# State space: moving sixteen token gathers one chunk later and splitting their statistics in two batches

## What is computed

```python
xn = x * rsqrt(mean(x * x) + EPS) * norm_w
xi, res = split(xn @ in_proj_w)
xi = silu(conv(xi) + conv_b)
delta, Bm, Cm = split(xi @ x_proj_w)
delta = softplus(delta @ dt_proj_w + dt_proj_b)
A = -exp(A_log)
# over the tokens of a sequence, 256 channels by 16 states:
state = exp(delta * A) * state + delta * Bm * xi
y = sum over states of state * Cm
out = (y + xi * D) * silu(res) @ out_proj_w + x
```

## Time and profile before

| what | value |
|---|---|
| median of 3 runs | 1254.69 us (1253.68 to 1259.11) |
| the profiled launch | 1261.0 us, its span 1259.1 us |
| DVE busy | 942.2 us (75%) |
| PE busy | 998.2 us (79%) |
| POOL busy | 830.8 us (66%) |
| ACT busy | 735.4 us (58%) |
| the state-space stage, first `dBu` to last `gate_rows` | 472.9 to 969.5 us |

### The profile page before, as it was taken

One profiled execution on the slowest core, in us unless ns is written; L12 is line 12 of the kernel. 1 busy time (PEld: TensorE's weight loads), 2 busy tenths in 40 slices (PEclk: granted clock), 3 DMA queues, 4 the chain that ended last, 5 costly groups with the idle time before them and its releaser, 6 DMA issues. The chain is left out here.

```text
span 1259.1 us, 17033 instructions
## 1 busy us (share of the span) xinstructions
PE 998.2 (79%) x4202; PEld 606.3 (48%) x4202; DVE 942.2 (75%) x2310; ACT 735.4 (58%) x1636; POOL 830.8 (66%) x604
## 2 busy tenths in 40 slices
PE   5888867489999978888888888898776335999970
PEld 4666755368888723333333333333222333777750
DVE  6999999653333437999898989999998743777760
ACT  4777747265555568776667676867531113777740
POOL 3333248557247275989898978787975077767676
PEclk9999989599999979999898989989989556999995
DMA  9993012246435343353544443444542014756543
GB/s 271 177 168 124 1 10 24 40 60 92 73 77 94 69 80 104 111 170 116 164 125 153 137 124 126 160 130 140 168 150 67 2 49 76 120 104 123 106 93 64
DMA packets 139137, 133.50 MB, mean 106 GB/s; under 512 B 14579, under 2 KB 120163, under 8 KB 138915
## 3 DMA queue, kind: packets, MB, share of 16 engines
q1 hardware_dynamic: 107106, 115.55, 34.2%
q0 software_dynamic: 31936, 16.86, 11.4%
HBM read 98.66 MB, written 31.60 MB: 103 GB/s over the span
## 5 line engine op out<-in xcount | busy, mean ns | idle before, releaser
L1871 POOL TENSOR_TENSOR ss_HC<-ss_Hs,ss_Cb 128x512 f32<-128x512 f32 x256 | 324.8, 1365 | 85.0 <-PE ss_Y L1621 64.4
L1621 PE MATMUL ss_Y<-ss_HC,g_ident 128*128 128x512 f32 x512 | 270.4, 649 | 47.3 <-POOL ss_HC L1871 41.0
L1915 DVE TENSOR_TENSOR_SCAN ss_Hs<-ss_dA,ss_dBu 128x512 f32<-128x512 f32 x256 | 296.8, 1200 | 7.7 <-ACT ss_dA L1781 7.7
L846 POOL DMA_INDIRECT rows<-m_XS,g_slot x128 | 174.3, 1362 | 61.7 <-issue 34.6
L1781 ACT ACTIVATE ss_dA<-ss_delta,g_A 128x510 f32<-128x510 f32 x256 | 168.3, 712 | 74.1 <-DVE ss_Hs L1915 73.9
L1621 PEld LDWEIGHTS ss_Y<-ss_HC,g_ident 128*128 128x128 f32 x512 | 92.9, 200 | 209.2 <-POOL ss_HC L1871 149.2
L1153 PE MATMUL m_x_UP<-g_m_w,m_x_gT 128*128 (+1 forms) x532 | 193.0, 469 | 0.0
L1907 DVE TENSOR_TENSOR ss_dBu<-ss_duP,ss_Bb 128x512 f32<-128x512 f32 x256 | 163.1, 682 | 10.5 <-DMA ss_Bb<-bc_rows 8.9
L1173 PEld LDWEIGHTS m_x_DP<-g_m_w,m_x_hT 128*128 128x128 f32 x908 | 121.9, 191 | 62.3 <-issue 34.6
L1173 PE MATMUL m_x_DP<-g_m_w,m_x_hT 128*128 (+1 forms) x908 | 140.7, 284 | 2.4 <-ACT m_x_hT L1245 2.3
L1245 ACT ACTIVATE m_x_hT<-m_x_HP 128x256 f32<-128x256 f32 (+1 forms) x188 | 80.3, 427 | 87.7 <-PE m_x_HP L1163 85.9
(11 more groups left out here) (271 smaller groups left out, 1760.9 us busy)
## 6 DMA issues: line engine op xcount, KB each, us to landing
ss_Bb<-bc_rows SPq DMA_DIRECT2D x64, 512.0 KB, 5.0
ss_Cb<-bc_rows SPq DMA_DIRECT2D x64, 512.0 KB, 4.1
rows<-g_Z SPq DMA_DIRECT2D x2, 5031.0 KB, 48.9
m_x_G<-rows SPq DMA_DIRECT2D x156, 64.5 KB
out_rows<-m_x_YO SPq DMA_DIRECT2D x156, 64.0 KB
g_m_w<-in_w_up SPq DMA_DIRECT2D x1, 2816.0 KB, 11.2
g_m_b<-in_b SPq DMA_DIRECT2D x1, 2160.0 KB, 10.3
g_X<-in_x SPq DMA_DIRECT2D x4, 512.0 KB, 5.8
```

Source lines behind the costliest of these rows:

```text
L846: self.nc.gpsimd.indirect_dma_start(self.XG, bass.IndirectOffsetOnAxis(self.rt.slot[k][:, t:t + 1], 0), self.XS[:, t, :], None, compute_op ...
L1621: ins = nc.tensor.matmul(Yp[:, h, :], ident[:], HC[n % 2][:, h, :], start=False, stop=n == N - 1)
L1871: nc.gpsimd.tensor_tensor(HC[n % 2][:, h, :], Hs[n % 4][:, h, :], Cb[g % 2][:, n % 2, :], ALU.mult).then_inc(hc_ready.sem, 1)
L1915: v_.tensor_tensor_scan(Hs[n % 4][:, h, :], dA[n % NA][:, h, :, :].rearrange("p s t -> p (s t)"), dBu[:, h, :], 0.0, ALU.mult, ALU.add).th ...
```

## The change

The 16 gathers of the last eight tiles move one chunk later. Before, POOL issued the eight with the first expert's rows in chunks 0 and 1 and the eight with the second expert's in chunks 2 and 3. Now tiles 24 to 27 get theirs in chunk 1 (first expert) and chunk 2 (second), and tiles 28 to 31 in chunks 3 and 4. The eight tiles become two batches of four, each with a semaphore of its own. The first has statistics at (4, 1), root at (4, 2), scales at (4, 3); the second has them at (5, 1), (5, 2) and (5, 3). SP's increment of a semaphore that nobody waits for, one per chunk, goes.

```diff
@@ state_space
-        gathered, late_gathered = m.sem("gathered"), m.sem("late_gathered")
-        soon, late = rows_of.batches[1], rows_of.batches[2]
-        n_soon, n_late = soon[1] - soon[0], late[1] - late[0]
-        sp_passed = m.sem("sp_passed")
+        gathered, late_gathered = m.sem("gathered"), [m.sem(f"late_gathered{q}") for q in range(2)]
+        soon, late = rows_of.batches[1], rows_of.batches[2:]
+        n_soon, n_late = soon[1] - soon[0], G
@@ SP
                     if back:
                         sp.wait_ge(bc_stored.sem, bc_stored.after(c + 1))
-                        sp.sem_inc(sp_passed, 1)
@@ ACT
-                        if (c, n) == (4, 2):
-                            rows_of.scalar_root(act, 2)
+                        if c in (4, 5) and n == 2:
+                            rows_of.scalar_root(act, c - 2)
@@ POOL
-                        i = 4 * c + (n - 8) // 2
-                        if n >= 8 and n % 2 == 0 and i < 2 * n_late:
-                            if i == n_late:
-                                pool.wait_ge(late_gathered, 16 * n_late)
-                            gather(i // n_late, late[0] + i % n_late, late_gathered)
+                        if 1 <= c <= 4 and n >= 8 and n % 2 == 0:
+                            q, k = divmod(c - 1, 2)
+                            if k == 1 and n == 8:
+                                pool.wait_ge(late_gathered[q], 16 * n_late)
+                            gather(k, late[q][0] + (n - 8) // 2, late_gathered[q])
@@ DVE
-                        if (c, n) == (4, 1):
-                            dve.wait_ge(late_gathered, 16 * 2 * n_late)
-                            rows_of.vector_stats(dve, 2, *late)
-                            rows_of.vector_moments(dve, 2)
-                        if (c, n) == (4, 3):
-                            rows_of.vector_scales(dve, 2)
+                        if c in (4, 5) and n == 1:
+                            dve.wait_ge(late_gathered[c - 4], 16 * 2 * n_late)
+                            rows_of.vector_stats(dve, c - 2, *late[c - 4])
+                            rows_of.vector_moments(dve, c - 2)
+                        if c in (4, 5) and n == 3:
+                            rows_of.vector_scales(dve, c - 2)
@@ build
-        state_rows = StateRows(nc, Maker(nc, outer, "sr_"), chain, X, mean, scales, ((0, HT), (HT, HT + 8), (HT + 8, T)))
+        state_rows = StateRows(nc, Maker(nc, outer, "sr_"), chain, X, mean, scales, ((0, HT), (HT, HT + 8), (HT + 8, HT + 12), (HT + 12, T)))
```

## The result

The changed kernel takes 1263.61 us in the median of 20 runs (1258.53 to 1271.88). The kernel before, run beside it, takes 1255.44 us (1252.41 to 1265.18, 20 runs). The ratio is 1.0051 with a 95% interval of 1.0034 to 1.0067: 6.4 us slower on 1254.69, or some 1261.1 us. The two medians lie 8.2 us apart, but each list spreads over 13 us, so I go by the ratio and its interval. The kernel is slower, since the interval leaves out 1. Whether by more than the 0.5% at which the prediction parted "slower" from "within" isn't decided: the ratio is just beyond it, and the interval holds it. The forecast was +5.7 us.

What follows compares the result with a forecast made beforehand. DVE was taken to bound the stage. Statistics in chunk 5 (+1.6) and the second root and scales (+4.1) made +5.7 us on 1254.69, so 1260.4 us, 0.45% slower; the range ran from 1255.5 to 1264.5.

Steps and rivals of the forecast that it cites:

- Chunk 0 buys nothing: Chunk 0: four gathers removed from POOL gain 0, since DVE never waited for POOL; bounds 0 and a 6.8 us gain.
- Chunks 1 to 3 at 0: Chunks 1 to 3: four gathers each as before and the same order on every engine, so 0 us.
- a sign against it: Periods of chunks 0 to 3 changing by over 1 us would show the prediction wrong.
- the moments are held up: Rival at (5, 1): POOL runs on through it and adds 3.2 us; +8.9, 1263.6 us; chance 0.10.
- Chunk 4, gathers hidden: Chunk 4, steps 8 to 14: four more POOL gathers hide under DVE's work; the sum is ready at 800.7.
- Statistics in chunk 5, +1.6: Chunk 5, step 1: statistics for a batch of four on DVE cost +1.6 us, bounds 0.4 and 2.5.
- POOL falls behind in chunk 4: Rival: PE's waits do not cover the first two gathers, sum 3.4 us later; +7.9, 1262.6 us; chance 0.15.
- Second root and scales, +4.1: Chunk 5, steps 2 and 3: 7.4 us on DVE, partly given back, leaving +4.1; bounds 2.5 and 7.4.
- chunks 6 and 7 keep their periods: Chunks 6 and 7: no change in their periods; all that follows the stage moves along.
- The sum: Whole kernel: 1.6 + 4.1 = +5.7 us, 1260.4 us, 0.45% slower.
- The port: Chunk 5's scales: blocked by POOL's instruction under the shared port rule, they stay at 2.8 us; without it 1.3.

Runs made afterwards that it cites:

- e2: The kernel before with the four gathers of chunk 0 left out (tiles 24 to 27 lack the first expert's rows); ratio 0.9997.
- e1: The changed kernel with its two batches, but every gather at its old step in chunks 0 to 3; ratio 1.0024 against the kernel before.
- e9: The kernel before with ACT's root behind its gate copy at (4, 3), DVE's scales at (4, 5) and chunk 6's normalise at step 5; ratio 0.9999.
- e3: The kernel before with four more gathers at steps 8 to 14 of chunk 4, into a tile nobody reads, without SP's increments; ratio 1.0011.
- e6: The changed kernel with both late roots ahead of the logarithm in ACT's step 2 instead of behind it; ratio 1.0052 against the kernel before.
- e10: The changed kernel with both late roots behind ACT's gate copy, scales and normalise at step 5 in chunks 4 and 5; ratio 1.0122 against the kernel before.
- e4: The changed kernel without the second root and second group of scales, chunk 7 normalised with constants; ratio 1.0038 against the kernel before.
- e11: The changed kernel without the second root only; the seven scale operations stay, chunk 7 uses chunk 6's numbers; ratio 1.0034 against the kernel before.
- e5: The kernel before with ACT's late root ahead of the logarithm in step 2 of chunk 4 instead of behind it; ratio 1.0007.
- e7: The kernel before with DVE's late scales at (4, 5) instead of (4, 3), and ACT's normalise of chunk 6 at step 5; ratio 1.0010.

## Why the prediction was nearly right

**Chunk 0 buys nothing.** Right. First `dBu` to first `gate_rows` took 78.21 us (548.15 - 469.94) instead of 78.44, and e2's ratio is 0.9997 with an interval that leaves out the 6.8 us.

**Chunks 1 to 3 at 0.** Wrong for chunks 1 and 2. The prediction had named a change of over 1 us there as a sign against it, and chunk 1 grew by 1.58. Chunks 1 and 2 together take 124.65 us after the change, and 124.64 to 124.78 in all four other launches that have both its gathers and its split. In six launches without that combination they take 122.62 to 122.81, e2 among them, and in two (e1, e9) 123.9. What goes with it in all thirteen launches is PE's clock. Here are the two chunks together, of the changed kernel, of e9 and of the kernel before:

```profile
548.15:672.80 124.65, 108.24 (x245) 43.79 (x246) 113.32 (x133) 83.41 (x125) 108.18 (x80) 0.92 0.44 137
```
```profile
551.36:675.28 123.92, 107.14 (x247) 43.51 (x246) 113.64 (x133) 84.87 (x128) 109.04 (x80) 0.93 0.46 141
```
```profile
551.33:674.14 122.81, 106.08 (x248) 44.04 (x248) 113.51 (x133) 85.16 (x128) 109.77 (x81) 0.94 0.46 140
```

A granted clock of 1.00 is 2.4 GHz throughout; less is a stretch with a part at 1.2 GHz. Summed from the clock's records, PE spends 20.5 us of the two chunks at 1.2 GHz in the five launches of 124.6 to 124.8 us, 17.1 in the two of 123.9 and 13.7 in the six of 122.6 to 122.8. DVE is busy for the same time in all (113.3 to 113.6 us), so the difference is waiting. Against the kernel before, most of it is one wait for B in the middle of chunk 1, 2.61 us instead of 1.15:

```profile
585.57 1.30 DVE L1905 TENSOR_TENSOR ss_dBu<-ss_duP,ss_Bb 128x512 f32<-128x512 f32 x2 [2.61 <-DMA ss_Bb<-bc_rows]
```
```profile
587.28 1.30 DVE L1907 TENSOR_TENSOR ss_dBu<-ss_duP,ss_Bb 128x512 f32<-128x512 f32 x2 [1.15 <-DMA ss_Bb<-bc_rows]
```

The rest is the wait for the sum, 3.57 instead of 3.21 us in chunk 1 and 3.48 instead of 3.08 in chunk 2. Against e2 it is the other way round: there the wait for B is 2.35 and the wait for the sum only 2.57. The eight `ss_HC` products before the next `gate_rows` show why, first in the changed kernel, then in the kernel before, then in e2:

```profile
599.46 5.76 PE L1619 MATMUL ss_Y<-ss_HC,g_ident 128*128 128x512 f32 x8 [1.87 <-POOL ss_HC L1869]
```
```profile
601.43 5.40 PE L1621 MATMUL ss_Y<-ss_HC,g_ident 128*128 128x512 f32 x8 [1.87 <-POOL ss_HC L1871]
```
```profile
608.35 4.79 PE L1621 MATMUL ss_Y<-ss_HC,g_ident 128*128 128x512 f32 x8 [1.89 <-POOL ss_HC L1871]
```

In the first two a part of the products runs at 1.2 GHz, in e2 none does. So where the slow stretches fall decides which wait grows, and how long they are in all goes with how long the chunks take. That the clock is the cause and no mere companion is argued from the products' times, not shown: no run sets it. The changed kernel and e2 have the same granted clock in each ten microseconds from 20 us before `gate_rows` to 50 us behind it, and PE is busy within 0.4 us of the same time in each. Why it then falls in one and not in the other isn't settled. e2 shows that fewer gathers in chunk 0 do not do it alone. e9, which before chunk 4 runs the same order of work as the kernel before, shows that one order can come out two ways.

In chunk 3's window, which holds the statistics of (4, 1), the 0 was right: 62.16 us against 62.38 and 62.12. But nothing came earlier, for the batch of four took 3.76 us to the next `dBu`, more than the 3.29 of the eight tiles before. Its L1408, which takes 0.17 us in chunk 5, took 2.42 here and ended at 733.70, with POOL's run of products (733.66). So the rival "the moments are held up" came true in a place where it cost nothing.

**Chunk 4, gathers hidden.** Right for the window (e3: 63.98 against 63.77, and no wait of DVE for the sum behind it). The sum was ready 64.1 us after `gate_rows` in the changed kernel and 63.9 in e3, against the forecast's 800.7 - 736.52 = 64.2. But the prediction asked only whether POOL would make `gate_rows` late. It didn't ask what else ran ahead of DVE at that point. e1 shows it: the second root is waited for 1.31 us without these gathers, and 3.98 with them.

**Statistics in chunk 5, +1.6.** Right: 1.52 in the row, +1.48 in the window, and the four other launches with the full change's gathers give 64.76 to 65.29. The moments ran free of POOL here, so that rival did not come true in chunk 5, though it was close: in e6 and e10 the same batch took 2.8 us there. The rival in which POOL falls behind in chunk 4 is out, because DVE didn't wait before `gate_rows` at 800.21.

**Second root and scales, +4.1.** The window met the forecast, 63.74 against 63.77. As a price it holds less well. Chunk 5 takes 58.4 to 60.7 us in the nine launches without a second root; against the closest two, e4 and e11, the root costs 5.0. Chunk 6 gives 1.5 back against them (1.3 and 0.7 against the two launches of the kernel before), which the prediction left out with "chunks 6 and 7 keep their periods". The net that e4 and e11 give is 3.3 us by the profiles; the timed runs give some 2 and can't tell it from 0. The prediction counted 2.8 us of scales behind 4.46 of waiting, both on DVE. The scales cost nothing once the root is gone (e11 against e4), and with the root first in ACT's queue the window is still 3.8 us longer than without it although DVE waits for no root (e6), so part of its price runs through PE and POOL, which wait for ACT. How the 5.0 us divide in the changed kernel itself isn't shown.

**The sum.** +5.7 was forecast and +6.4 measured, with an interval of 4.3 to 8.4. It is close in part because two misses cancel: some 1.8 too little in chunks 1 and 2, and some 1.3 too much from chunk 6. That they cancel is luck. The forecast lay 0.6 us under the bound of 0.5% and the measurement 0.1 above it, both less than either miss.

**The port.** The blocked scales came as written: L1424 ended with POOL's instruction at 813.5. The Trainium skill (SBUF — State Buffer, section "Who interferes with whom") has the rule that DVE and GpSimd share a port pair, and that a DVE operation with two SBUF inputs or in a two-port mode waits until the GpSimd instruction in progress ends. The rows of e10 agree: L1424, whose inputs both lie in SBUF, ended at 817.93, with the POOL instruction ahead of the product at 817.86. They add that the wait comes anew with each small operation.

No version beat the kernel before: e5, e7 and e9 lie within 0.1% of it, and their intervals hold 1.

## What to carry to other kernels

A step that is split in two pays its fixed parts twice: here the table load and the root, in the queue of an engine whose later work others wait for. Price it in that engine's queue, by asking who waits for what stands behind it, and not only by the wait for its own result. A transfer that is hidden still uses up the lead of the engine that issues it, so look for what that lead was paying for. Put chains of tiny DVE operations where GpSimd is idle: moving seven of them by two steps turned 3.3 us into 8.6 in e10, and 2.8 into 4.9 in e7.

## What the runs showed of the hardware that was not expected

- A chain of tiny DVE operations does not take its turn once but once for each operation. Seven of them took 1.26 us in chunk 0, where POOL was not in the way, 3.25 with one POOL instruction in the way and 8.6 us beside a POOL without a gap (e10). RECIPROCAL took 0.17 us in e10 while POOL's instruction ran on around it, and never more than 0.26 in this stage.
- TensorE's granted clock over the same ten microseconds of the same work was 0.83 in the changed kernel and 1.00 in e2, whose load up to then was nearly the same, and eight products took 5.76 or 4.79 us. Over chunks 1 and 2, 20.5, 17.1 and 13.7 us at 1.2 GHz went with 124.7, 123.9 and 122.7 us in thirteen launches. In this stage that is worth one to two microseconds of the whole, as much as the single terms of the sum.
